# A four-image metaformer on one core: attention of image 1 one lead-in step earlier, and a residual addition on GpSimd

## What is computed

```python
# attention: value, query, key, off are depthwise 3x3 convolutions of the normalized x
o = gelu(layernorm(off) * ln_g + ln_b)
pos = tanh(einsum('bhwc,pc->bhwp', o, w_off2) + ref)
v_sampled = grid_sample_bilinear(value, pos)
attn = einsum('bcm,bcn->bmn', query, key) * SCALE
x = x + einsum('bchw,oc->bohw', einsum('bmn,bcn->bcm', attn, v_sampled), w_out)
# FFN, 4 experts, the 2 best gated, on each pixel's 96 channels
t = t + sum_e gate_e * (gelu(ln(t) @ w1[e] + b1[e]) @ w2[e] + b2[e])
x = x + depthwise convolutions(ln(x))        # 7x7, 5x3, 3x5 and two separable ones
t = t + FFN(ln(t))                           # second set of weights
```

## Time and profile before

| what | value |
|---|---|
| median of three runs | 1548.86 us |
| the profiled execution | 1553.49 us, span 1551.7 us |
| FFN starts (first chunk of (0,0)) | 195.84 us into the span |
| (0,0) and (0,1) | 27.22 and 24.54 us |
| first steps of slots 1, 2, 3, 4 | 28.16, 28.56, 24.13 and 27.89 us |
| slots 4 to 7 | 958.30 us to the end |
| mean granted TensorE clock | 0.965 |

### The profile page before, as it was taken

The page is one execution under the profiler, slowest core; times in us unless marked ns, Lnnn a source line. Parts: engine busy times, 40 slices in busy tenths (PEclk is TensorE's granted clock), DMA queues, the critical chain, the costliest instruction groups (busy, mean ns, idle before and its releaser), DMA issues.

```text
span 1551.7 us, 21475 instructions
## 1 busy us (share of the span) xinstructions
PE 1408.4 (91%) x6700; PEld 1053.1 (68%) x6700; DVE 1135.1 (73%) x2875; ACT 725.3 (47%) x1508; POOL 517.0 (33%) x533
## 2 busy tenths in 40 slices
PE   5879688997899999998789999999999999998998
PEld 4656655664556776665556676778888788877786
DVE  6956988699875444489994555686888786799787
ACT  5633353455433444556443444454545454456454
POOL 5051162111810000120360001463346433465575
PEclk9998799998899999999999999999999999999999
DMA  5632235323524222424144212362324322221121
GB/s 125 138 111 68 50 109 150 107 70 83 143 62 118 74 57 71 132 79 113 49 121 125 59 49 50 95 161 59 91 68 125 94 57 69 75 72 55 56 75 53
DMA packets 169602, 136.53 MB, mean 88 GB/s; under 512 B 115120, under 2 KB 162258, under 8 KB 169394
## 3 DMA queue, kind: packets, MB, share of 16 engines
q1 hardware_dynamic: 164514, 129.91, 30.9%
q0 software_dynamic: 3072, 4.82, 1.2%
q10 hardware_dynamic: 1904, 0.43, 0.1%
HBM read 95.47 MB, written 39.30 MB: 87 GB/s over the span
## 4 chain that ended last, share of the span: by engine, by line
PE 56%; issue 16%; DVE 13%; POOL 8%; ACT 6%; SPq 1%; DMA 0%; ACTq 0%; POOLq 0%; DVEq 0%
PE at_ps L1376 10%; PE y_ps L1231 9%; PE h_ps L1238 6%; PE h_ps L1240 6%; PE h_ps L1239 6%; PE y_ps L1220 4%; POOL pix_mem L1109 3%; PE y_ps L1221 3%; PE y_ps L1222 3%; DVE vq_mem L1581 3%; POOL ln_rstd L1082 3%; PE at_ps L1298 2%; ACT ln_cen L895 2%; PE lb_ps L1193 2%; DVE part L1537 2%
## 5 line engine op out<-in xcount | busy, mean ns | idle before, releaser
L1037 ACT ACTIVATE hidden<-h_ps,b 128x448 f32<-128x448 f32 x609 | 384.1, 633 | 609.9 <-PE h_ps L1240 596.2
L1238 PE MATMUL h_ps<-xh,w1h 96*128 96x448 f32 x672 | 366.4, 545 | 5.1 <-ACT pix_mem L940 2.6
L1082 POOL TENSOR_TENSOR ln_rstd<-ln_ve,minus_half 112x4 f32<-112x4 f32 x112 | 166.4, 1486 | 610.0 <-DVE ln_ve L1520 595.5
L1231 PE MATMUL y_ps<-hidden,w 128*96 128x448 f32 x672 | 323.0, 566 | 19.6 <-ACT hidden L1037 13.2
L1537 DVE SCALAR_TENSOR_TENSOR part<-y_ps,b,gate_t 96x448 f32<-96x448 f32 x224 | 151.4, 676 | 203.1 <-PE y_ps L1231 155.3
L1101 POOL CAST in_w<-hidden 128x448 fp32r<-128x448 f32 x273 | 200.2, 737 | 244.4 <-ACT hidden L1037 162.4
L1239 PE MATMUL h_ps<-xl,w1h 96*128 96x448 f32 x672 | 249.8, 372 | 0.0
L1240 PE MATMUL h_ps<-xh,w1l 96*128 96x448 f32 x672 | 249.0, 370 | 0.0
L1238 PEld LDWEIGHTS h_ps<-xh,w1h 96*128 96x128 f32 x672 | 129.8, 193 | 91.9 <-issue 59.5
L1239 PEld LDWEIGHTS h_ps<-xl,w1h 96*128 96x128 f32 x672 | 131.6, 196 | 66.7 <-issue 61.3
L1581 DVE SCALAR_TENSOR_TENSOR vq_mem<-x_mem,all_w,vq_mem 128x770 f32<-128x770 f32 (+1 forms) x168 | 163.7, 1016 | 1.9 <-POOL ln_rstd L1082 0.7
(11 more groups left out here) (186 smaller groups left out, 2123.6 us busy)
## 6 DMA issues: line engine op xcount, KB each, us to landing
gate_t<-gates_dram SPq DMA_DIRECT2D x112, 336.0 KB, 3.3
value_pairs<-pix_mem SPq DMA_DIRECT2D x56, 168.0 KB, 3.2
x_mem<-norm_c SPq DMA_DIRECT2D x16, 420.0 KB, 4.5
x_mem<-norm_a SPq DMA_DIRECT2D x14, 336.0 KB, 4.0
res<-x_attn SPq DMA_DIRECT2D x28, 168.0 KB, 3.0
x_ffn<-ffn_out SPq DMA_DIRECT2D x28, 168.0 KB, 2.0
ln_x<-x_ffn SPq DMA_DIRECT2D x28, 168.0 KB, 3.1
norm_c<-ln_cm SPq DMA_DIRECT2D x28, 168.0 KB, 3.6
```

Source lines behind the costliest of these rows:

```text
L1037: act.activation(to[:, :], h_ps[c % H_BANKS][:, 0:TILE], ACT.Gelu, bias=b1[l][:, c:c + 1]).then_inc(gelu_done, 1)
L1082: pool.tensor_tensor(ln_rstd[n % 2][:, :], ln_ve[n % 2][:, :], minus_half[0:SUB, 0:NSUB], ALU.pow)\
L1231: pe.matmul(y_ps[e % Y_BANKS][0:C, 0:TILE], w2[l][:, c, :], hidden[c % HID_RING][:, :], start=(j == 0), stop=(j == CPE - 1)).then_inc(hid_ ...
L1238: pe.matmul(ps, hi, xh[:, ring(k)], start=True, stop=False)
```

## The change

It has two parts. In the first, stages 0, 1 and 2 of image 1's attention stand in lead-in steps 11, 12 and 13 instead of 12, 13 and 14, and its stage 3 in step 14 holds nine of the 27 query taps, which stood in (0,0) and (0,1). The products with the key (KEY_CONV, KEY_TAKE) stand a step later in the lead-in. Eight gathers of image 1 end the lead-in where there were four. In the second part, the residual's addition of slots 0 to 3 (28 tiles) is an instruction of POOL, `pool_residual`, that stands in the step after its tile, behind the power of that step's first job; the last tile of slot 3 has it at the end of its own step. `sum_experts` writes into `pair` in place of `part`. `combine` 0 then waits only for the tile before to be summed up to its pairs.

```diff
-START_ATTN = {5: [(0, 0)], ..., 10: [(0, 5)], 11: [(0, 6)],
-              12: [(1, 0)], 13: [(1, 1)], 14: [(1, 2)]}
+START_ATTN = {5: [(0, 0)], ..., 10: [(0, 5)], 11: [(0, 6), (1, 0)],
+              12: [(1, 1)], 13: [(1, 2)], 14: [(1, 3)]}
...
-        Q_ROUNDS = ({4: (0, 5), 5: (5, 8), 6: (8, 9)}, {4: (0, 5), 5: (5, 9)})
+        Q_ROUNDS = ({4: (0, 5), 5: (5, 8), 6: (8, 9)}, {3: (0, 3), 4: (3, 7), 5: (7, 9)})
...
-        KEY_CONV = {..., (1, 1, 4): 0, (1, 1, 5): 1, (1, 1, 7): 2}
+        KEY_CONV = {..., (1, 2, 1): 0, (1, 2, 2): 1, (1, 3, 2): 2}
...
+            def pool_residual(u, m):
+                k = TILES * u + m
+                pool.wait_ge(summed, 3 * k + 2)
+                pool.wait_ge(res_ld, 16 * (k + 1))
+                if m > 0:
+                    pool.wait_ge(ffn_st[u], 16 * m)
+                elif u > 0:
+                    pool.wait_ge(ffn_st[u - 1], 16 * TILES)
+                pool.tensor_tensor(ffn_out[:, :], pair[0:C, 0, :], res[:, :], ALU.add).then_inc(summed, 1)
...
                 if 0 in jobs:
                     scale_rows(jobs[0])
+                if slot >= 0 and (slot, p) != (0, 0):
+                    pool_residual(*divmod(TILES * slot + p - 1, TILES))
                 if 3 in stages and stages[3] == 0:
                     gather(0, 4, 8)
...
                 if 2 in stages and stages[2] in ON_PE:
-                    gather(stages[2], 0, 4)
+                    gather(stages[2], 0, 4 if stages[2] == 0 else 0)
...
+                if (slot, p) == (SPLIT_SLOTS[0] - 1, TILES - 1):
+                    pool_residual(slot, p)
...
-                if e == 0:
-                    dve.wait_ge(summed, 3 * k)
+                if e == 0 and k > 0:
+                    dve.wait_ge(summed, 3 * k - 2)
...
             def sum_pairs(u, m):
                 k = TILES * u + m
                 dve.wait_ge(y_used, Y_BANKS + E * (k + 1))
+                dve.wait_ge(summed, 3 * k)
...
-                dve.tensor_tensor(part[:, 0, :], pair[0:C, 0, :], pair[0:C, 1, :], ALU.add).then_inc(summed, 1)
+                dve.tensor_tensor(pair[0:C, 0, :], pair[0:C, 0, :], pair[0:C, 1, :], ALU.add).then_inc(summed, 1)
 
             def sum_residual(u, m):
+                if u < SPLIT_SLOTS[0]:
+                    return
...
-            TAPS_LEAD = {0: dict(none, combine2=1, end=1), 1: dict(none, combine0=5, combine1=3, combine2=4, end=3)}
+            TAPS_LEAD = {0: dict(none, combine0=3, combine1=3, combine2=3, end=3), 3: dict(none, end=1), 1: dict(none, combine0=5, combine1=3, combine2=4, end=3)}
```

More of the change, by code:

```diff
@@ L80 @@
               (3, 1): [("c1", 6)], (3, 2): []}
-START_ATTN = {5: [(0, 0)], 6: [(0, 1)], 7: [(0, 2)], 8: [(0, 3)], 9: [(0, 4)], 10: [(0, 5)], 11: [(0, 6)],
-              12: [(1, 0)], 13: [(1, 1)], 14: [(1, 2)]}
-LEAD_Y = {(11, 5): 0, (11, 6): 1, (11, 7): 2, (11, 9): 3, (12, 0): 4, (12, 3): 5, (12, 7): 6, (12, 9): 7}
-LEAD_ADD = {(11, "combine1"): (0, 1), (11, "combine2"): (2,), (11, "combine3"): (3,), (12, "normalize0"): (4,),
-            (12, "combine1"): (5,), (12, "combine2"): (6,), (12, "combine3"): (7,)}
+START_ATTN = {5: [(0, 0)], 6: [(0, 1)], 7: [(0, 2)], 8: [(0, 3)], 9: [(0, 4)], 10: [(0, 5)], 11: [(0, 6), (1, 0)],
+              12: [(1, 1)], 13: [(1, 2)], 14: [(1, 3)]}
+LEAD_Y = {(11, 5): 0, (11, 6): 1, (11, 7): 2, (11, 9): 3, (11, 10): 4, (12, 0): 5, (12, 3): 6, (12, 5): 7}
+LEAD_ADD = {(11, "combine1"): (0, 1), (11, "combine2"): (2,), (11, "combine3"): (3,), (11, "end"): (4,),
+            (12, "normalize0"): (5,), (12, "combine0"): (6,), (12, "combine1"): (7,)}
 ON_PE = {0: ("off", "query", "key", "query"), 1: ("off", "key")}
@@ L480, in metaformer_kernel @@
         QUERY_TAKE = {(0, 11): (0, 0), (1, 2): (0, 1), (2, 11): (0, 2), (3, 8): (1, 0), (3, 11): (1, 1), (4, 5): (1, 2)}
[L481 to L482 removed]
+        KEY_CONV = {(0, 2, 11): 0, (0, 3, 0): 1, (0, 3, 1): 2, (1, 2, 1): 0, (1, 2, 2): 1, (1, 3, 2): 2}
+        KEY_TAKE = {(0, 3, 0): 0, (0, 3, 1): 1, (0, 3, 3): 2, (1, 2, 2): 0, (1, 2, 3): 1, (1, 3, 4): 2}
         DIAG_AT = {(4, 11): ("query", 0), (5, 1): ("query", 1), (5, 4): ("query", 2), (5, 8): ("key", 0),
@@ L995, in attention @@
                         take_conv(b, "key", 0, KEY_TAKE[b, stage, c])
-                    if (stage, c) == ((2, 10) if b == 0 else (4, 1)):
+                    if stage == 2 and c == (10 if b == 0 else 11):
                         tanh_pos(b)
@@ L1135, in _ @@
                 if 4 in stages and stages[4] > 0:
-                    gather(stages[4], *((4, 8) if stages[4] in ON_PE else (8, 12)))
+                    gather(stages[4], 8, 12)
                 if 1 in jobs:
@@ L1145, in _ @@
                 if 2 in stages and stages[2] in ON_PE:
-                    gather(stages[2], 0, 4)
+                    gather(stages[2], 0, 4 if stages[2] == 0 else 0)
                 if 3 in stages and stages[3] == 0:
                     gather(0, 8, 12)
-                if 3 in stages and stages[3] not in ON_PE:
+                if 3 in stages and stages[3] > 0:
                     gather(stages[3], 0, 8)
                 if 4 in stages and stages[4] > 0:
-                    gather(stages[4], 8 if stages[4] in ON_PE else 12, 2 * GQ)
+                    gather(stages[4], 12, 2 * GQ)
+                if (slot, p) == (SPLIT_SLOTS[0] - 1, TILES - 1):
+                    pool_residual(slot, p)
         @block.tensor
@@ L1557, in sum_residual @@
                     dve.wait_ge(ffn_st[u - 1], 16 * TILES)
-                dve.tensor_tensor(ffn_out[:, :], part[:, 0, :], res[:, :], ALU.add).then_inc(summed, 1)
+                dve.tensor_tensor(ffn_out[:, :], pair[0:C, 0, :], res[:, :], ALU.add).then_inc(summed, 1)
             def taps3(out_ap, in_ap, n, g, at, step, stride):
@@ L1598, in attn_taps @@
                     lists = [taps3(key[:, g, :], srcs[g], 1, g, at["key"] + g, 3, 2) for g in range(G)]
-                if stage > 3 and "query" in at:
+                if stage in Q_ROUNDS[b == 1] and "query" in at:
                     lists = [taps3(query[:, g, :], srcs[g], 3, g, at["query"] + g, 3, 1)[q0:q1] for g in range(G)]
```

## The result

The changed kernel takes 1568.06 us (median of 4 runs, 1564.07 to 1568.47); the kernel before, run beside it, 1549.16 (1548.81 to 1550.23). The ratio is 1.0115 [1.0097, 1.0133], some +18 us against the +5.3 forecast. The profiled execution took 1564.07 us (span 1562.2), that of before 1553.49. A second profile of the changed kernel, taken later, is of a run of 1573.32 us (span 1571.5).

A forecast was written before the change was run, and what follows sets the result against it. PE carries most of the chain of waits, DVE bounds some steps, and gate loads ("issue") bound slot starts. -8.0 - 2.0 + 14.8 + 0.5 = +5.3 us on 1548.86 gives 1554.2 us; range 1546 to 1561.

The forecast's parts named there:

- part A: Lead-in and slot 0: image 1's earlier attention takes taps and waiting out of slot 0; -8.0 us, bounds -5 and -10.
- B: First steps of slots 1 to 3: gate loads wait behind a store that waits for GpSimd's addition; +14.8 us, +11 to +18.
- Rival (2): Slot 0 and lead-in: the relief wins, gates landing in about 3.3 us; -3.0 us, 1545.9 us; chance 0.27.
- The stall of 3.02 us: PE's wait for `ln_cen` at 213.65, its power queued behind gathers on GpSimd; half, 1.5 us, taken as returned.
- The wait for `part` at 252.16: PE's wait of 2.52 us for DVE, placed late in (0,1); expected gone.
- rival (4): Lead-in: DVE's waits only move, nine taps delay the FFN's start or slot 0's first combine about 5 us; 1559.2 us; chance 0.13.
- C: Tiles 3 to 5 of slots 0 and 2: the residual's addition off DVE, half paid back as blocking; -2 us, -4 to +1.
- Rival (3): DVE and GpSimd block each other, additions costing DVE more than they free; +2.3 us there, 1558.5 us; chance 0.15.
- D: Step (4,0): slot 3's last residual on GpSimd plus a handover, `combine` 0 waiting for gates; +0.5 us, 0 to 1.5.

The follow-up runs named there:

- e2: The kernel before with the residual's addition of slots 0 to 3 on GpSimd, the attention where it was: 1568.1 us, ratio 1.0118.
- e3: e2 with the last tile of each slot added on DVE again, 24 of 28 additions staying on GpSimd: 1551.09 us, ratio 1.0000.
- e7: e2 with the gate loads of a slot's first tile ahead of the last store of the slot before: 1551.43 us, ratio 1.0003.
- e5: e1 with four of the eight gathers of lead step 14 put behind the power of (0,0): 1543.29 us, ratio 0.9954.
- e1: The changed kernel with the residual's addition back on DVE, so the attention's move alone: 1551.92 us, ratio 1.0006.

## Why the prediction had the direction right and the size wrong

The time lies 7 us above the top of the stated range, 1561. The step that failed is part A: the forecast took 8 us off for it, and alone it measures +1.

**B held in its mechanism, and in the profiles in its size.** Counted from its slot's start, `combine` 0 was forecast at 21.8 us in (1,0) (409.2 against 387.4), 20.1 in (2,0) and 20.5 in (3,0). It came at 412.12 - 390.32 = 21.8, 19.3 and 21.1. The steps between are there too, of GpSimd and of SP's queue in (1,0):

```profile
403.10 0.97 POOL L1119 DMA_INDIRECT pix_mem<-value_pairs,o_idx  x1 [0.31 <-issue]
404.10 1.05 POOL L1082 TENSOR_TENSOR ln_rstd<-ln_ve,minus_half 112x4 f32<-112x4 f32 x1
405.14 1.12 POOL L1111 TENSOR_TENSOR ffn_out<-pair,res 96x448 f32<-96x448 f32 x1
```

```profile
406.28 0.30 SPq L693 DMA_DIRECT2D x_ffn<-ffn_out  x1
406.68 0.90 SPq L684 DMA_DIRECT2D gate_t<-gates_dram  x2
```

The power behind the eighth gather at 1.05 us (forecast 1.05), the addition 1.12 (1.0), the gates issued 0.42 after it (0.42), and `combine` 0 begins 412.12 - 406.68 = 5.44 us after that (5.16). Only the figure in the last paragraph of the prediction, 5 to 8 us of idle ahead of `combine` 0, was under its own sum: 10.2 and 9.7 came. Rival (2), the gates landing in 3.3 us, fell with it. The timed cost of the addition alone (`e2`) is 18 us, with an interval from 13.5 to 23, which leaves it open whether it is more than B's 11.5 to 16.4 in the profiles; `e3` and `e7` show that it comes by the gates. Steps after a longer wait at a lower clock (last section) may add to it, but that I have not measured apart.

**A failed, and at two steps.** (1) "Four gathers fewer stand there": I counted the gathers of slot 0 and overlooked that lead-in step 14 now issues eight instead of four, on the same queue, ahead of the power of (0,0). The stall of 3.02 us was to halve; it doubled to 5.94. Some relief did come in (0,1): 24.54 fell to 20.29, and PE is busy for 20.12 of that. But it isn't from the wait that I had named. In (0,1) PE had waited 0.49 us for the gates' scores, and 1.21 and 2.00 for a layer norm; 0.17 is left of these. The longest of them, before:

```profile
238.69 0.59 PE L1193 MATMUL lb_ps<-ident,ln_cen 112*96 112x112 f32 x4 [2.00 <-ACT ln_cen L895]
```

The wait for `part` at 252.16 lies 4.6 us into the stretch of (0,2), not in (0,1). In its place the changed kernel waits 1.89 us for the load of `ln_x` in profile 1, and 0.79 for that load and 1.05 for `part` in profile 2, so little of the 2.52 came back there. The relief was eaten by (0,0), 27.22 to 32.34. `e5` undoes the eight gathers alone and comes near the forecast: 51.8 - 46.0 = 5.8 us in two steps. The 2.7 in (0,2) (38.68 to 35.95, at a granted clock of 0.96 and of 1.00) aren't the gathers': `e1` has them too (35.98).

(2) "FFN's first tile doesn't wait for that end; I leave its start where it is": taps filled DVE's idle time by being put ahead of sums for which PE waited. That is rival (4), which had the place right and 5 us for it; 4.5 and 1.9 came. It took A at -3 since it, too, let the relief in slot 0 stand. `e1` measures A as a whole at +1 us, between -2 and +4, so this term is off by some 9 us (6 to 12) of the miss of 13.

**C was -2 and is nothing that the runs show** (`e7`: between -1.5 and +2.6 us). (0,3) and (0,4) didn't move in either profile (19.90 and 20.59 before, 19.87 and 20.57 after): PE is the bound there, busy for 19.43 of 19.89 us of (0,3) in profile 2. For (0,5) `e3` has the same granted clock, 0.94, as before; its stretch and PE's wait in it, and then PE's wait in the kernel before:

```profile
326.21:356.19 29.98, 24.87 (x121) 16.98 (x120) 27.58 (x79) 20.12 (x36) 3.13 (x3) 0.94 0.45 122
```

```profile
334.28 0.86 PE L1261 MATMUL at_ps<-ident,vq_mem 128*112 128x128 f32 x3 [2.62 <-DVE vq_mem L1596]
```

```profile
335.30 0.89 PE L1249 MATMUL at_ps<-ident,vq_mem 128*112 128x128 f32 x3 [3.07 <-DVE vq_mem L1581]
```

29.98 instead of 30.14 us: of the 0.62 us taken off DVE 0.45 shorten one wait of PE, and a third of that is left at the end. The addition was put at 1.0 us; it takes 1.69 on average (28 of them, by line and shape), and from 1.12 to 5.61:

```profile
L1111 POOL TENSOR_TENSOR ffn_out<-pair,res 96x448 f32<-96x448 f32 x28 | 47.3, 1689 | 30.6 <-DVE pair L1563 30.6
```

```profile
829.72 5.61 POOL L1111 TENSOR_TENSOR ffn_out<-pair,res 96x448 f32<-96x448 f32 x1 [13.62 <-DVE pair L1563]
```

The 5.61 stands beside five taps of DVE, 829.56 to 834.32, which take 4.76 us, the 0.95 each of taps in a row: there GpSimd stood and DVE didn't. Elsewhere DVE stood as well. Two products of `kon_mem` in (3,1) on DVE, in the kernel before and in the changed kernel, and GpSimd's addition beside the latter:

```profile
799.74 1.94 DVE L1729 TENSOR_TENSOR kon_mem<-pix_mem,o_cw 98x768 f32<-98x768 f32 x2
```

```profile
814.15 2.76 DVE L1746 TENSOR_TENSOR kon_mem<-pix_mem,o_cw 98x768 f32<-98x768 f32 x2
```

```profile
812.67 3.42 POOL L1111 TENSOR_TENSOR ffn_out<-pair,res 96x448 f32<-96x448 f32 x1
```

By the pages DVE is busy for 1135.1 us before and 1124.2 in the changed kernel. The 28 additions were 17.4 us of it, so 6.5 came back as longer instructions; every profile without additions on GpSimd has 1135.1 to 1136.1, every one with all 28 1124.2 to 1126.9. The prediction took half of the freed time as paid back, and 6.5 of 17.4 is not far from it. What failed is the expectation that the rest shows at the end of the slot. Rival (3), in which the additions cost DVE more than they free, fell: 6.5 is less than 17.4. By the lock of the Trainium skill's SBUF — State Buffer, "Who interferes with whom", the second comer stands; the trace agrees in order, GpSimd having come second at 829.72 and DVE at 814.15, though GpSimd stood through five taps and not one.

**D** was +0.5 and came out at -0.4 and -0.6: too small to matter.

So the forecast's sum failed in the gains. With A at +1, C at 0 and B and D as forecast it would have been +16, close to the +18 measured.

## What to carry to other kernels

On every in-order queue, list what will stand ahead of the next consumer after the move, and take it from that queue's order around the place, not from the count of the stage that gets lighter. Handing an instruction to another engine hands over the semaphore it raises, and with it every transfer queued behind the waiting store; here four of 28 small additions cost 18 us. Idle time of an engine is cover only for work that stands behind the sums that another engine waits for; put ahead of them, the same taps moved the idle time instead of filling it.
